# Softmax row sums of an attention kernel: nine of 32 score tiles summed by DMA instead of seven, none directly by TensorE

## The chip, the cores and the metric

The kernel runs on one core of a Trainium2 chip. TensorE does the matrix products into PSUM, ScalarE the exponentials, VectorE additions and copies, GpSimd here issues DMAs that add while they move, SyncE issues the other DMAs. The metric is the device time of one execution in microseconds; the time before is the median of three runs.

## The reference

The input is two images of 256 channels and 64 x 64 positions. Layer 0 is attention with 8 heads of 32 channels over all 4096 positions; layer 1 is a pooled non-local block. The change touches layer 0 alone:

```python
qkv = einsum('oc,bchw->bohw', w_qkv, x)          # q, k, v: (2, 8 heads, 32, 4096)
scores = einsum('bhdi,bhdj->bhij', q, k) / sqrt(32)
attn = softmax(scores, axis=-1)
out = einsum('bhij,bhdj->bhdi', attn, v)
x = einsum('oc,bchw->bohw', w_proj, out) + x      # then layer 1
```

The kernel takes the exponentials without subtracting a maximum, multiplies them with the values, and divides by their sums at the end. The sums over j are what the change is about.

## The kernel before

Layer 0 runs once for each image and each group g of four heads, so four times; call each a stage. In a stage the 4096 query positions are cut into NC = 8 chunks of 512 columns, and the 4096 key positions into JT = 32 tiles of 128 rows. One step makes one score tile of 128 x 2048 (four heads side by side), so there are 256 steps in a stage and 1024 in all.

For each tile TensorE computes the scores (line 372, twelve fp16 products in three terms). The first head goes to the PSUM bank `lead`, the other three to one of two banks of three. ScalarE takes the exponentials in two instructions, line 458 for `lead` and line 459 for the other three, and writes them to one of RING = 8 slots of `P`. TensorE may compute the scores of tile n+2 only when line 458 of tile n+1 has emptied `lead` (line 418). After the scores of each step come four fp32 products a tile with the values (line 381) into the PSUM bank `both`.

The values start late in each chunk, since `both` is used first to make the sums of the chunk before. PV_FROM = 3 says that steps 0, 1 and 2 of a chunk do no values; PV_MORE lists six steps that do three halves of a tile instead of two, so that the values are complete at step 31.

The sums of a chunk are gathered in three ways. VectorE adds 24 tiles into `acc`, in 23 instructions (line 490, the first takes two tiles). The seven tiles of SUM_D are added into `accD` by DMA: GpSimd issues two DMAs a tile, one for each half (k = 0 and 1), the first tile as a plain copy (line 512) and the others with an addition (line 515). Each half waits for the same half of the tile before it (`s_dma[k]`, line 514). GpSimd works in order, so the first half of the next tile is not issued before the second half of this one has been. Tile 31 is not added anywhere. At step 0 of the next chunk TensorE multiplies `acc` with a matrix of ones (line 391), at step 1 tile 31 (line 398), at step 2 `accD` (line 406). Before line 391 VectorE must have copied the finished output out of `both` (line 467, `s_o_free`), and after line 406 it copies the sums to `L` (line 473), before the values of the next chunk may start (`s_l_free`).

ScalarE writes a slot of the ring again eight tiles later. It waits until the values and the adding of the tile are done, for a tile of SUM_D until both its DMAs have landed (lines 440 to 451).

Of the kernel before, what the change touches and what calls it, by code (L numbers as in the profile page):

```python
# [16 lines left out]
HEADS, D = 8, 32  # L17
G = 4
# [3 lines left out]
JT = N // 128  # L22
# [16 lines left out]
RING = 8  # L39
LAG = 2  # L40
SUM_D = [3, 7, 11, 16, 20, 24, 29]
SUM_PE = JT - 1
SUM_V = [j for j in range(SUM_PE) if j not in SUM_D]
ADDS = len(SUM_V) - 1
PV_FROM = 3
PV_MORE = [9, 10, 17, 18, 25, 26]

# [15 lines left out]
def conv_seq(nc, x, wqkv, wproj, gw, tw, pw, ww, vectors, biases, out, r_dram, r1_dram):  # L63
# [3 lines left out]
    with ExitStack() as root:  # L67
# [30 lines left out]
        ones = sb(root, "ones", [128, D])  # L98
# [111 lines left out]
        def layer0(b):  # L210
            with ExitStack() as ctx:
# [8 lines left out]
                for g in range(NG):  # L220
# [123 lines left out]
                    with ExitStack() as c2:  # L344
# [16 lines left out]
                        with nc.Block() as block:  # L361
                            @block.tensor
                            def _(pe):
# [22 lines left out]

                                def sums_of_acc(c):
                                    pe.wait_ge(s_o_free, c + 1)
                                    pe.wait_ge(s_add, (c + 1) * ADDS)
                                    for h in range(G):  # L390
                                        last = nc.tensor.matmul(both[h * D:(h + 1) * D, :], ones[:], acc[:, h, :],  # L391
                                                                start=True, stop=False)
                                    last.then_inc(s_sum, 1)

                                def sums_of_tile(c):
                                    r = (c * JT + SUM_PE) % RING * G
                                    for h in range(G):
                                        last = nc.tensor.matmul(both[h * D:(h + 1) * D, :], ones[:], P[:, r + h, :],
                                                                start=False, stop=False)
                                    last.then_inc(s_sum, 1)  # L400

                                def sums_of_dma(c):
                                    for k in range(2):
                                        pe.wait_ge(s_dma[k], 16 * len(SUM_D) * (c + 1))
                                    for h in range(G):
                                        last = nc.tensor.matmul(both[h * D:(h + 1) * D, :], ones[:], accD[:, h, :],
                                                                start=False, stop=True)
                                    last.then_inc(s_sum, 1)
# [5 lines left out]
                                for n in range(NC * JT + PV_FROM):  # L414
# [5 lines left out]
                                    elif n < NC * JT:  # L420
                                        pe.wait_ge(s_exp, 2 * n + 2)
                                    if i == 0 and c:
                                        sums_of_acc(c - 1)
                                    if i == 1 and c:
                                        sums_of_tile(c - 1)
                                    if i == 2 and c:
                                        sums_of_dma(c - 1)
                                    if c < NC:
# [11 lines left out]
                            def _(act):  # L440
                                def slot_free(m):

                                    c, j = divmod(m, JT)
                                    act.wait_ge(s_pv, m + 1)
                                    if j in SUM_D:
                                        for k in range(2):
                                            act.wait_ge(s_dma[k], 16 * (c * len(SUM_D) + SUM_D.index(j) + 1))
                                    elif j == SUM_PE:
                                        act.wait_ge(s_sum, c * 3 + 2)
                                    else:  # L450
                                        act.wait_ge(s_add, c * ADDS + adds_through(j))
# [12 lines left out]
                            def _(dve):  # L464
# [4 lines left out]
                                def sums_out(c):  # L469
                                    dve.wait_ge(s_sum, (c + 1) * 3)  # L470
                                    if c:
# [3 lines left out]
                                for c in range(NC):  # L475
                                    if c:
                                        output_out(c - 1)
                                    for n in range(ADDS):
                                        j = SUM_V[n + 1]
                                        dve.wait_ge(s_exp, 2 * (c * JT + j) + 2)  # L480
                                        r = (c * JT + j) % RING * G
                                        if n == 0:
                                            if c:
                                                dve.wait_ge(s_sum, (c - 1) * 3 + 1)
                                            r0 = (c * JT + SUM_V[0]) % RING * G
# [4 lines left out]
                                        nc.vector.tensor_tensor(acc[:], old, P[:, r:r + G, :], ALU.add).then_inc(s_add, 1)  # L490
                                        if n == 0 and c:
                                            sums_out(c - 1)
                                        if n == ADDS // 2 and c:
# [7 lines left out]
                            def _(pool):  # L501
                                for c in range(NC):
                                    for i, j in enumerate(SUM_D):
                                        for k in range(2):
# [4 lines left out]
                                            if i == 0:  # L509
                                                if c:  # L510
                                                    pool.wait_ge(s_sum, c * 3)
                                                nc.gpsimd.dma_start(dst, src).then_inc(s_dma[k], 16)  # L512
# [606 lines left out]
```

## Time and profile before

| What | Before |
|---|---|
| median of 3 runs (lowest, highest) | 2709.13 us (2707.6, 2714.66) |
| the profiled execution's own time | 2712.51 us |
| its span in the trace | 2710.8 us |
| TensorE busy | 2553.2 us, 94% |
| ScalarE busy | 2223.1 us, 82% |
| VectorE busy | 2162.7 us, 80% |
| DMA queue of GpSimd, share of 16 engines | 42.7% |

A busy share says how long an engine had an instruction in hand, not that the engine sets the pace. Times are microseconds from the start of the span. In a row of the timeline stand the start, the duration, the engine, the line, the operation, what is written and read, how many instructions were merged (x8), and in brackets how long the engine had stood idle and what ended that. In this kernel a product in fp32 shows as two records, so x8 at line 381 are the four products of one tile. PE is TensorE, DVE VectorE, ACT ScalarE and POOL GpSimd.

### The profile page before, as it was taken

Reading aid. Unit: us, or ns where it says so; the run is one execution under the profiler, and the core shown is the slowest. Engines: PE = TensorE matmul, PEld = TensorE weight load, DVE = VectorE, ACT = ScalarE, POOL = GpSimd, SP = SyncE. Lnnn points to the kernel's source line nnn. Section 1 sums busy time; section 2 is a strip of 40 time slices with the busy share of each in tenths; the row PEclk is TensorE's granted clock in tenths of the full one; section 3 lists DMA queues with packets and bytes.
Section 4 is the critical chain, followed back from the end, with each engine's and each line's share of the span. In section 5 each row is a group of like instructions: output and inputs, shape, how many; then the busy total and the mean of one; then the engine's idle time right before and its main releaser. Section 6 shows DMA issues by size and latency. Waiting matters only on the chain. (4 is left out here: it accounts for less than half of the span.)

```text
span 2710.8 us, 58233 instructions
## 1 busy us (share of the span) xinstructions
PE 2553.2 (94%) x24658; PEld 747.2 (28%) x24666; DVE 2162.7 (80%) x1414; ACT 2223.1 (82%) x2490; POOL 403.5 (15%) x588
## 2 busy tenths in 40 slices
PE   7999999989999999698979999999899999995999
PEld 4222222242222222243442222222422222222434
DVE  3889999948899999586538999999489999994864
ACT  4999999949999999237439999999499999991474
POOL 0111111101111111011001111111011111110100
PEclk9999999999999999899989999999999999998999
DMA  2556666605566566201115665665056656652011
GB/s 83 110 126 126 126 125 127 126 17 110 126 124 127 121 127 126 86 11 48 41 69 117 126 128 121 127 126 121 16 121 124 128 121 127 127 121 79 11 51 43
DMA packets 89277, 272.03 MB, mean 100 GB/s; under 512 B 17504, under 2 KB 18592, under 8 KB 88608
## 3 DMA queue, kind: packets, MB, share of 16 engines
q0 software_dynamic: 64512, 234.91, 42.7%
q1 hardware_dynamic: 24480, 33.16, 3.6%
q8 instruction: 199, 3.26, 0.5%
q14 instruction: 86, 0.70, 0.1%
HBM read 22.88 MB, written 8.68 MB: 12 GB/s over the span
## 5 line engine op out<-in xcount | busy, mean ns | idle before, releaser
L490 DVE TENSOR_TENSOR acc<-acc,P 128x2048 f32<-128x2048 f32 x704 | 1613.4, 2292 | 83.2 <-ACT P L459 15.3
L459 ACT ACTIVATE P<-scores 128x1536 f32<-128x1536 f32 x1024 | 1594.8, 1557 | 0.0
L381 PE MATMUL psOL<-P,V 128*32 128x512 f32 (+1 forms) x8960 | 1074.3, 567 | 1.4 <-ACT P L459 1.4
L372 PE MATMUL psOL<-Q,K 32*128 32x512 f16 x3072 | 842.7, 380 | 28.0 <-ACT P L458 17.3
L372 PE MATMUL scores<-Q,K 32*128 32x512 f16 x9216 | 849.2, 380 | 0.0
L458 ACT ACTIVATE P<-psOL 128x512 f32<-128x512 f32 x1024 | 711.9, 695 | 36.9 <-PE scores L372 36.9
L515 POOL DMA_DIRECT2D accD<-P x384 | 335.7, 998 | 1231.9 <-ACT P L459 1022.4
L372 PEld LDWEIGHTS psOL<-Q,K 32*128 32x128 f16 x3072 | 207.5, 93 | 986.0 <-ACT P L458 855.7
L381 PEld LDWEIGHTS psOL<-P,V 128*32 128x32 f32 x8960 | 196.9, 108 | 474.4 <-issue 438.5
L372 PEld LDWEIGHTS scores<-Q,K 32*128 32x128 f16 x9216 | 220.8, 93 | 0.0
L253 PE MATMUL scores<-X,wq_sb 128*128 128x512 f32 x256 | 128.1, 631 | 40.5 <-DMA X<-in_x 28.1
L512 POOL DMA_DIRECT2D accD<-P x64 | 35.2, 556 | 681.0 <-ACT P L459 398.7
L1039 DVE SCALAR_TENSOR_TENSOR Pl<-O,Ph 128x1536 f16<-128x1536 f32 (+1 forms) x48 | 75.9, 1581 | 65.8 <-ACT Ph L1012 65.8
L490 DVE TENSOR_TENSOR acc<-P 128x2048 f32<-128x2048 f32 x32 | 73.3, 2292 | 64.7 <-PE psOL L391 35.2
L1005 ACT ACTIVATE O<-scores 128x1536 f32<-128x1536 f32 (+1 forms) x48 | 62.4, 1300 | 71.1 <-PE scores L940 71.1
L750 PE MATMUL scores<-O,wp_sb 128*128 128x512 f32 x128 | 62.4, 633 | 49.8 <-DVE O L707 49.8
L739 ACT ACTIVATE Yh<-X 128x512 f16<-128x512 f32 x32 | 20.1, 630 | 104.9 <-DVE X L727 104.9
L952 PE MATMUL psOL<-Ph,GTh 128*128 128x512 f16 x256 | 97.1, 379 | 0.0
L952 PE MATMUL psOL<-Pl,GTh 128*128 128x512 f16 x256 | 97.1, 379 | 0.0
L952 PE MATMUL psOL<-Ph,GTl 128*128 128x512 f16 x256 | 97.1, 379 | 0.0
L253 PEld LDWEIGHTS scores<-X,wq_sb 128*128 128x128 f32 x256 | 51.7, 204 | 100.8 <-issue 70.9
L305 DVE SCALAR_TENSOR_TENSOR Q<-scores,Q 128x512 f16<-128x512 f32 x32 | 22.1, 691 | 66.3 <-ACT Q L284 66.3
(113 smaller groups left out, 1499.3 us busy)
## 6 DMA issues: line engine op xcount, KB each, us to landing
accD<-P POOLq DMA_DIRECT2D x448, 512.0 KB, 5.2
X<-in_x SPq DMA_DIRECT2D x16, 512.0 KB, 7.1
R<-att_inv SPq DMA_DIRECT2D x32, 256.0 KB
out<-res SPq DMA_DIRECT2D x32, 256.0 KB, 2.0
R<-pool_inv SPq DMA_DIRECT2D x2, 2048.0 KB, 7.1
TB<-TA SPq DMA_DIRECT2D x2, 512.0 KB, 4.6
wq_sb<-in_w_qkv SPq DMA_DIRECT2D x1, 768.0 KB, 4.4
Ls<-L SPq DMA_DIRECT2D x32, 8.0 KB
```

Source lines behind the costliest of these rows:

```text
L253: last = nc.tensor.matmul(slot(u), w, X[:, t, c * CH:(c + 1) * CH], start=(t == 0), stop=(t == CT - 1))
L372: last = nc.tensor.matmul(dst[h], K[rows, kp, j * 128:(j + 1) * 128], Q[rows, qp, cs], start=(n == 0), stop=(n == 2))
L381: last = nc.tensor.matmul(both[h * D:(h + 1) * D, lo:hi], V[:, j, h * D:(h + 1) * D], P[:, r + h, lo:hi], start=(j == 0), stop=(j == JT - 1))
L458: nc.scalar.activation(P[:, r, :], lead, ACT.Exp, scale=SCORE).then_inc(s_exp, 1)
L459: nc.scalar.activation(P[:, r + 1:r + G, :], bank[n % 2].rearrange("p (u n) -> p u n", n=CH), ACT.Exp, scale=SCORE).then_inc(s_exp, 1)
L490: nc.vector.tensor_tensor(acc[:], old, P[:, r:r + G, :], ALU.add).then_inc(s_add, 1)
L512: nc.gpsimd.dma_start(dst, src).then_inc(s_dma[k], 16)
L515: nc.gpsimd.dma_start(dst, src, accum_op=ALU.add).then_inc(s_dma[k], 16)
L750: last = nc.tensor.matmul(slot(u), wp_sb[:, k, t * 128:(t + 1) * 128], O[:, k, c * CH:(c + 1) * CH], start=(k == 0), stop=(k == CT - 1))
L952: last = nc.tensor.matmul(psOL[:, t * CH:(t + 1) * CH], w[:, m, ts], v[:, p, m, :], start=(n == 0), stop=(n == 3 * MT - 1))
L1005: nc.scalar.activation(P32[:, p, ms, :], bank[o % 2][:, 0:SZ[k] * CH].rearrange("p (u n) -> p u n", n=CH), ACT.Exp, scale=SCORE1).then_inc ...
L1039: nc.vector.scalar_tensor_tensor(out=Pl[:, p, ms, :], in0=P32[:, p, ms, :], scalar=PS, in1=Ph[:, p, ms, :], op0=ALU.mult, op1=ALU.subtract ...
```

## The change

`SUM_D` has nine tiles now, mostly three apart where they were four or five apart. VectorE adds the other 23 tiles, tile 31 among them, in 22 instructions. TensorE makes two sums between chunks instead of three: `accD` at step 0 and `acc` at step 1. The values start at step 2 and four steps, 9, 10, 19 and 20, carry three halves. VectorE copies the sums to `L` before its first addition of the chunk, where it used to do it after.

```diff
--- before.py
+++ after.py
@@ -38,12 +38,11 @@
 
 RING = 8
 LAG = 2
-SUM_D = [3, 7, 11, 16, 20, 24, 29]
-SUM_PE = JT - 1
-SUM_V = [j for j in range(SUM_PE) if j not in SUM_D]
+SUM_D = [4, 7, 10, 13, 17, 20, 23, 26, 29]
+SUM_V = [j for j in range(JT) if j not in SUM_D]
 ADDS = len(SUM_V) - 1
-PV_FROM = 3
-PV_MORE = [9, 10, 17, 18, 25, 26]
+PV_FROM = 2
+PV_MORE = [9, 10, 19, 20]
 
 
 def adds_through(j):
@@ -384,26 +383,19 @@
                                     if hi == CH:
                                         last.then_inc(s_pv, 1)
 
-                                def sums_of_acc(c):
+                                def sums_of_dma(c):
                                     pe.wait_ge(s_o_free, c + 1)
-                                    pe.wait_ge(s_add, (c + 1) * ADDS)
-                                    for h in range(G):
-                                        last = nc.tensor.matmul(both[h * D:(h + 1) * D, :], ones[:], acc[:, h, :],
-                                                                start=True, stop=False)
-                                    last.then_inc(s_sum, 1)
-
-                                def sums_of_tile(c):
-                                    r = (c * JT + SUM_PE) % RING * G
-                                    for h in range(G):
-                                        last = nc.tensor.matmul(both[h * D:(h + 1) * D, :], ones[:], P[:, r + h, :],
-                                                                start=False, stop=False)
-                                    last.then_inc(s_sum, 1)
-
-                                def sums_of_dma(c):
                                     for k in range(2):
                                         pe.wait_ge(s_dma[k], 16 * len(SUM_D) * (c + 1))
                                     for h in range(G):
                                         last = nc.tensor.matmul(both[h * D:(h + 1) * D, :], ones[:], accD[:, h, :],
+                                                                start=True, stop=False)
+                                    last.then_inc(s_sum, 1)
+
+                                def sums_of_acc(c):
+                                    pe.wait_ge(s_add, (c + 1) * ADDS)
+                                    for h in range(G):
+                                        last = nc.tensor.matmul(both[h * D:(h + 1) * D, :], ones[:], acc[:, h, :],
                                                                 start=False, stop=True)
                                     last.then_inc(s_sum, 1)
 
@@ -420,11 +412,9 @@
                                     elif n < NC * JT:
                                         pe.wait_ge(s_exp, 2 * n + 2)
                                     if i == 0 and c:
+                                        sums_of_dma(c - 1)
+                                    if i == 1 and c:
                                         sums_of_acc(c - 1)
-                                    if i == 1 and c:
-                                        sums_of_tile(c - 1)
-                                    if i == 2 and c:
-                                        sums_of_dma(c - 1)
                                     if c < NC:
                                         at, end = halves_by(i - 1), halves_by(i)
                                         while at < end:
@@ -445,8 +435,6 @@
                                     if j in SUM_D:
                                         for k in range(2):
                                             act.wait_ge(s_dma[k], 16 * (c * len(SUM_D) + SUM_D.index(j) + 1))
-                                    elif j == SUM_PE:
-                                        act.wait_ge(s_sum, c * 3 + 2)
                                     else:
                                         act.wait_ge(s_add, c * ADDS + adds_through(j))
 
@@ -467,7 +455,7 @@
                                     nc.vector.tensor_copy(O[:, g, c * CH:(c + 1) * CH], both).then_inc(s_o_free, 1)
 
                                 def sums_out(c):
-                                    dve.wait_ge(s_sum, (c + 1) * 3)
+                                    dve.wait_ge(s_sum, (c + 1) * 2)
                                     if c:
                                         dve.wait_ge(s_out, 16 * c)
                                     nc.vector.tensor_copy(L[:], both).then_inc(s_l_free, 1)
@@ -475,21 +463,20 @@
                                 for c in range(NC):
                                     if c:
                                         output_out(c - 1)
+                                        sums_out(c - 1)
                                     for n in range(ADDS):
                                         j = SUM_V[n + 1]
                                         dve.wait_ge(s_exp, 2 * (c * JT + j) + 2)
                                         r = (c * JT + j) % RING * G
                                         if n == 0:
                                             if c:
-                                                dve.wait_ge(s_sum, (c - 1) * 3 + 1)
+                                                dve.wait_ge(s_sum, c * 2)
                                             r0 = (c * JT + SUM_V[0]) % RING * G
                                             old = P[:, r0:r0 + G, :]
                                         else:
                                             dve.wait_ge(s_add, c * ADDS + n)
                                             old = acc[:]
                                         nc.vector.tensor_tensor(acc[:], old, P[:, r:r + G, :], ALU.add).then_inc(s_add, 1)
-                                        if n == 0 and c:
-                                            sums_out(c - 1)
                                         if n == ADDS // 2 and c:
                                             dve.wait_ge(s_out, 16 * c)
                                             nc.vector.reciprocal(Ls[:, g, c - 1:c, :], Ls[:, g, c - 1:c, :]
@@ -508,7 +495,7 @@
                                             pool.wait_ge(s_exp, 2 * (c * JT + j) + 2)
                                             if i == 0:
                                                 if c:
-                                                    pool.wait_ge(s_sum, c * 3)
+                                                    pool.wait_ge(s_sum, c * 2 - 1)
                                                 nc.gpsimd.dma_start(dst, src).then_inc(s_dma[k], 16)
                                             else:
                                                 pool.wait_ge(s_dma[k], 16 * (c * len(SUM_D) + i))
```

The order of TensorE's instructions around the first change of chunk, before. Rows at line 372 are scores, L381 values; "..." stands for the other scores.

```order
L381 MATMUL psOL<-P,V 32x512 x4
...
L391 MATMUL psOL<-acc,ones 32x512 [waits s_add,s_o_free]
...
L398 MATMUL psOL<-P,ones 32x512 x4
...
L406 MATMUL psOL<-accD,ones 32x512 [waits s_dma1,s_dma0]
...
L381 MATMUL psOL<-P,V 32x512 [waits s_l_free]
```

And now, where scores are at line 371 and values at line 380:

```order
L380 MATMUL psOL<-P,V 32x512 x4
...
L391 MATMUL psOL<-accD,ones 32x512 [waits s_dma1,s_dma0,s_o_free]
...
L398 MATMUL psOL<-acc,ones 32x512 [waits s_add]
...
L380 MATMUL psOL<-P,V 32x512 [waits s_l_free]
```

The wait for the two DMA semaphores moved from step 2 to step 0, the wait for the last addition from step 0 to step 1, and the product with tile 31 is gone.

VectorE's instructions from the first chunk's additions to the second's, before (`acc<-P` is the first addition of a chunk):

```order
L490 TENSOR_TENSOR acc<-acc,P 128x2048 [waits s_add,s_exp] x22
L467 COPY O<-psOL 128x512 [waits s_pv]
L490 TENSOR_TENSOR acc<-P 128x2048 [waits s_sum,s_exp]
L473 COPY L<-psOL 128x512 [waits s_sum]
L490 TENSOR_TENSOR acc<-acc,P 128x2048 [waits s_add,s_exp] x11
```

And now:

```order
L479 TENSOR_TENSOR acc<-acc,P 128x2048 [waits s_add,s_exp] x21
L455 COPY O<-psOL 128x512 [waits s_pv]
L461 COPY L<-psOL 128x512 [waits s_sum]
L479 TENSOR_TENSOR acc<-P 128x2048 [waits s_sum,s_exp]
L479 TENSOR_TENSOR acc<-acc,P 128x2048 [waits s_add,s_exp] x11
```

One addition a chunk is gone, and the copy to `L` now stands ahead of the first one.

## Rows read from the trace of the kernel before

**Rows 1.** The page: busy time of each engine, and the DMA queues.

```profile
PE 2553.2 (94%) x24658; PEld 747.2 (28%) x24666; DVE 2162.7 (80%) x1414; ACT 2223.1 (82%) x2490; POOL 403.5 (15%) x588
q0 software_dynamic: 64512, 234.91, 42.7%
```

**Rows 2.** Two chunks: stretch, length, busy time of each engine, clock, DMA.

```profile
137.45:197.32 59.87, 59.73 (x696) 13.70 (x688) 54.11 (x27) 59.13 (x65) 11.62 (x14) 1.00 0.62 125
197.32:257.19 59.87, 59.73 (x696) 13.68 (x688) 54.12 (x27) 59.13 (x65) 11.67 (x14) 1.00 0.61 125
```

**Rows 3.** Timeline of ScalarE over a change of chunk and a pair of long steps.

```profile
187.36 1.50 ACT L459 ACTIVATE P<-scores 128x1536 f32<-128x1536 f32 x1
190.49 0.69 ACT L458 ACTIVATE P<-psOL 128x512 f32<-128x512 f32 x1
...
194.11 0.74 ACT L458 ACTIVATE P<-psOL 128x512 f32<-128x512 f32 x1
...
203.14 0.87 ACT L458 ACTIVATE P<-psOL 128x512 f32<-128x512 f32 x1
...
208.61 0.90 ACT L458 ACTIVATE P<-psOL 128x512 f32<-128x512 f32 x1
...
212.98 0.60 ACT L458 ACTIVATE P<-psOL 128x512 f32<-128x512 f32 x1 [0.25 <-PE scores L372]
```

**Rows 4.** Timeline of TensorE over the same change of chunk.

```profile
190.16 1.07 PE L381 MATMUL psOL<-P,V 128*32 128x512 f32 x8
...
192.04 1.06 PE L391 MATMUL psOL<-acc,ones 128*32 128x512 f32 x8
193.07 0.39 PE L372 MATMUL psOL<-Q,K 32*128 32x512 f16 x1
...
193.82 1.07 PE L398 MATMUL psOL<-P,ones 128*32 128x512 f32 x8
```

**Rows 5.** Timeline of VectorE over the same change of chunk.

```profile
183.04 7.08 DVE L490 TENSOR_TENSOR acc<-acc,P 128x2048 f32<-128x2048 f32 x3
191.29 0.69 DVE L467 COPY O<-psOL 128x512 f32<-128x512 f32 x1 [1.17 <-PE psOL L381]
```

**Rows 6.** Timeline of GpSimd: tile 29, then tiles 16 and 20 later.

```profile
185.49 1.77 POOL L515 DMA_DIRECT2D accD<-P  x2 [7.25 <-ACT P L459]
...
280.58 1.75 POOL L515 DMA_DIRECT2D accD<-P  x2 [7.81 <-ACT P L459]
287.96 0.86 POOL L515 DMA_DIRECT2D accD<-P  x1 [5.63 <-ACT P L459]
289.71 0.87 POOL L515 DMA_DIRECT2D accD<-P  x1 [0.89 <-DMA accD<-P]
```

**Rows 7.** Issue to landing: tile 29 of two chunks, a late second half, all L512.

```profile
DMA to landing us min/median/max: 4.6/5.6/6.6
DMA to landing us min/median/max: 4.6/6.3/8.1
DMA to landing us min/median/max: 6.1/6.1/6.1
DMA to landing us min/median/max: 2.9/3.9/6.1
```

**Rows 8.** Two stretches that each hold one tile's pair of adding DMAs.

```profile
212.40:218.40 6.00, 6.00 (x76) 1.33 (x72) 5.79 (x3) 5.75 (x7) 0.50 (x1) 1.00 0.95 180
222.00:228.00 6.00, 5.99 (x80) 1.57 (x76) 5.90 (x4) 5.80 (x7) 0.47 (x1) 1.00 0.96 179
```

**Rows 9.** Timeline of the end of the last stage.

```profile
2437.02 1.75 POOL L515 DMA_DIRECT2D accD<-P  x2 [7.83 <-ACT P L459]
2444.32 1.07 PE L406 MATMUL psOL<-accD,ones 128*32 128x512 f32 x8
2445.44 0.69 DVE L473 COPY L<-psOL 128x512 f32<-128x512 f32 x1 [3.18 <-PE psOL L406]
```

## The prediction

> **What bounds the kernel now.** I read the busy shares first, then two chunks side by side, then ScalarE's timeline, then the other engines' across one change of chunk, and last the DMAs that GpSimd issues. TensorE is busy 94% of the span and ScalarE 82% [rows 1], which does not yet say which of them sets the pace. Inside a stage the chunks repeat to the hundredth: 59.87 us each, TensorE busy 59.73, ScalarE 59.13, VectorE 54.1 [rows 2]. ScalarE's start of line 458 is the beat. From 190.49 to 203.14 it beats seven times, 1.807 us a step, with no idle time named [rows 3]: ScalarE is the bound, and this stretch holds all three sums of the chunk before. 32 such steps are 57.83 us, so a chunk has 2.04 us beyond ScalarE's pace. They come from the long steps: over one pair ScalarE goes from 208.61 to 212.98, 4.37 us for two steps, and the idle time there is ended by the scores [rows 3]. Three pairs share the 2.04 us, 0.68 us a pair (the pair shown loses 0.76, a little of which comes back after it). So TensorE counts in the long steps and at the change of chunk if something holds it there, and nowhere else.
>
> **What the change takes away.** One pair of long steps goes: 32 chunks x 0.68 = 21.8 us. The product with tile 31 goes as well, 1.07 us in the records [rows 4]. It gives nothing between chunks, because it lies in a step without values, under ScalarE's beat of 1.807; at the end of each stage, where nothing covers it, it is worth about 1 us, and I count it in the tail below. VectorE loses one addition a chunk, 2.36 us (7.08 for three) [rows 5]. It has 5.8 us idle a chunk already (59.87 less 54.1) and gives nothing directly.
>
> **What it moves: the wait for the DMA.** The product with `accD` stood at step 2 and stands at step 0. Tile 29, the last one of SUM_D, is the same tile as before. Its DMAs were issued at 185.49, when ScalarE had finished it [rows 6], and the product that stood at step 0 began at 192.04 [rows 4], 6.55 us later. Nothing makes ScalarE finish tile 29 earlier relative to step 0. So the question is when tile 29's second half lands. It is issued 0.88 us behind the first (1.77 us for two issues) [rows 6] and lands 6.6 us after its issue in the shortest usual case and 8.1 in the longer one [rows 7]; over the 32 tiles 29 of the trace the mean is 7.1, the two rows being examples of the two kinds (16 of 32 are at 6.6 to 6.8, 12 at 7.2 to 8.3). That is 7.5 us after the first issue at the usual best and 8.0 on the mean, against the 6.55 us at which TensorE arrives. A new stall at step 0 is 1.45 us on the mean even if the DMAs never queue.
>
> Of that stall ScalarE has little to give. At 194.11 line 458 takes 0.74 us where one that waited takes 0.60 [rows 3]: some 0.15 us of reserve. TensorE's own order has none, since the next scores follow the sum at once (192.04 + 1.03 = 193.07) [rows 4], and ScalarE's later steps run at its own pace, so nothing is caught up. Behind the waiting product on TensorE stand the scores of tile 3; for these waits ScalarE, and for ScalarE everything. Cost without queueing: 1.3 us a change of chunk, and 0.8 if every landing is at 7.5.
>
> **What it adds: a tighter chain of DMAs.** The tiles of SUM_D were 4 or 5 steps apart, 7.2 us or more; now seven of the eight gaps are 3 steps, 5.42 us, and two of those (10 to 13, 20 to 23) hold a pair of long steps, 6.1 us. What can the DMA engines do? In the two stretches of 6.00 us, each around one tile's two adding DMAs, the engines' share is 0.95 and 0.96 [rows 8]: 5.7 us of all 16 engines a tile, at 180 GB/s. As a cross-check, the queue's 42.7% of 2710.8 us is 1157 us for 192 adding tiles and 32 plain ones [rows 1]; at 2.6 for a plain one, taken as half, 5.6 remain for an adding one. A gap of 5.42 against a service of 5.6 means that the DMAs are never ahead. Tile 13 to 17 (7.2 us) clears what has gathered; after it come 17, 20, 23, 26, 29. With a service of 5.6 the lag at tile 29 is 0.3 us. The longer landings weigh more: on the mean a second half takes 0.5 us over the usual 6.6. If that is engine time the service is 6.1, and the lag is 0.7 + 0 + 0.7 + 0.7, about 2.0 us. The trace has cases of a late second half: at 289.71 it is issued 1.75 us behind the first half instead of 0.88 and lands in 6.1 [rows 6, 7], where a pure queue of 5.6 would make it 5.7. So part of the extra remains under queueing, and I take 1.0 us, the middle of 0.3 and 2.0. That gives 1.3 + 1.0 = 2.3 us a change of chunk, with ends of 0.8 and 3.3; there are 7 changes in each of four stages, 28 in all: 64 us, ends 22 and 92.
>
> A page of the Trainium skill speaks against this. "DMA: Bandwidth & Descriptors", section "Anatomy of one DMA — SWDGE (gpsimd) path", gives 2.0 us and the bytes at 436 GB/s for a DMA issued by GpSimd, which for 512 KB is an estimate of 3.2 us. The plain copies agree with it at their shortest (2.9 us), the adding ones do not (4.6 us and more) [rows 7]. By the page both halves would be home long before step 0, and the sum would be the second rival's; by the rows it is mine.
>
> **VectorE at the change of chunk.** Now the last addition is tile 31's. It can start only when tile 30's is done: ScalarE finishes tile 31 at 188.86 (187.36 + 1.50) and tile 30 a step earlier, at 187.05 [rows 3], two additions end at 187.05 + 4.7 = 191.8, the copy of the output takes 0.7 more, and the product could start at 192.5 instead of 192.04. VectorE will not be further behind than that: its additions start right behind the copy to `L`, 22 x 2.36 + 0.3 = 52.2 us after it, and a chunk is 59.2 us or longer. This 0.45 us lies under the wait for the DMA (ready 1.4 us late or more). If that cover is gone it costs 0.3 us a chunk after ScalarE's reserve. The new place of the copy to `L` costs nothing: it follows the last sum by the same 0.1 us and the values wait for it as before, one step earlier. The ring: tile 29's slot is needed 7 steps, 12.6 us, after its exponentials, and the landing with lag is at 8.9, up to 9.9.
>
> **Ends of stages.** In the last stage tile 29 is issued at 2437.02, the last sum begins at 2444.32, the copy to `L` ends at 2446.13 [rows 9]. Now the landing is at 2437.0 + 8.9 = 2445.9, then come two products (2.0 us) and the copy (0.8): 2448.7, 2.6 us later, ends 1.2 and 3.6. Four stages: +10 us, ends 5 and 14.
>
> **Sum.** -21.8 + 64 + 10 = +53 us. The profiled execution took 2712.5 (span 2710.8); it would take 2766. It lies 3.4 us above the median of the runs, so in medians: 2709.1 + 53 = 2762 us, ends 2709 - 22 + 22 + 5 = 2714 and 2709 - 22 + 92 + 14 = 2793.
>
> **Rivals.**
> First, *landings at their best*. Every second half lands 6.6 us after its issue and queueing absorbs the rest: 0.8 us a change, +22 + 5 - 22, so 2714 us, no change. For it: half of the tiles 29 land so. Against it: three in eight take 0.6 us more or longer, and the next tiles come sooner.
> Second, *the DMA is home in time*, faster. If a half that is issued alone or in a steady chain lands in under 5.5 us, the product at step 0 waits only for VectorE: -22 + 28 x 0.3 = -13, 2696 us. It decides if the landing is under 6.7 us after tile 29's first issue; no pair in the trace does it. This is also what the page's figure would give.
> Third, *the chain becomes the bound*, slower still. If each second half needs its full 6.6 us from issue to landing, however the halves are staggered, the lag grows 1.2 us a gap (0.5 where long steps lie) and from tile 17 on reaches about 4.2 us, some 5.3 if the plain gap does not clear it: 1.3 + 4.2 to 5.3, or 6 us a change, 168 - 22 + 25, 2880 us. For it: second halves issued late still take 6.1 us. Against it: they take less than 6.6, and the share of 0.95 says that the engines work through.
>
> **Chances and range.** The forecast, with its own range 2718 to 2800 (the ends of the sum, less the first rival's own place): 0.70. First rival 0.12, second 0.07, third 0.11. What a measurement of this kernel can tell from no change is about 0.3%, 8 us. The forecast, the third rival and a small part of the first (over 2717) are slower: 0.83; same 0.10; faster 0.07. The range that holds 8 in 10 leaves out the second rival and most of the third: 2710 to 2825.
>
> **What would show it.** TensorE's product with `accD` idles before it, ended by the DMA, 1 to 3 us in 28 places, and ScalarE has an equal gap ended by scores once a chunk; a chunk is 61.5 us instead of 59.87. GpSimd's waits at line 502 (the old 515) are ended by the DMA most of the time. ScalarE's gaps at long steps are 4 a chunk, not 6. If no idle time stands before the product, or if the chunk is 59.2 us, my landing time is wrong; if the chunk is over 64 us, the third rival is right. A stall ended by the output's copy would make VectorE the cause.

## The result, and the profile after

| | Before | After |
|---|---|---|
| median | 2711.89 us (4 runs, 2707.6 to 2714.97) | 2806.62 us (4 runs, 2801.51 to 2808.12) |
| ratio to before, 95% interval | | 1.0347 (1.0332 to 1.0361) |
| span of the profiled execution | 2710.8 us | 2805.7 us |
| mean granted clock | 0.983 | 0.968 |

The kernel is 94.7 us slower. The prediction was 2762 us with a range to 2825: the direction holds and so does the main cause, a wait for the DMA at step 0, but the loss is nearly twice as large as the 53 us forecast.

The page of the kernel after, with the busy times, the DMA queue and the groups that answer to the argument (busy us, mean ns, then idle time before them and what ended it):

```profile
PE 2563.2 (91%) x24146; PEld 735.5 (26%) x24154; DVE 2086.7 (74%) x1382; ACT 2221.8 (79%) x2490; POOL 511.0 (18%) x716
q0 software_dynamic: 82944, 302.03, 54.0%
L446 ACT ACTIVATE P<-psOL 128x512 f32<-128x512 f32 x1024 | 706.5, 690 | 109.9 <-PE scores L371 109.9
L461 DVE COPY L<-psOL 128x512 f32<-128x512 f32 x32 | 22.1, 691 | 190.0 <-PE psOL L398 190.0
L391 PE MATMUL psOL<-accD,ones 128*32 128x512 f32 x256 | 43.8, 760 | 90.1 <-DMA accD<-P 90.1
```

VectorE has less to do than before [rows 1]. TensorE idles 90.1 us in front of the product with `accD`, ended by the DMA every one of 32 times. ScalarE waits 109.9 us for scores; before it was 36.9:

```profile
L458 ACT ACTIVATE P<-psOL 128x512 f32<-128x512 f32 x1024 | 711.9, 695 | 36.9 <-PE scores L372 36.9
```

Two neighbouring chunks, to be read beside [rows 2]:

```profile
141.16:203.89 62.73, 60.43 (x680) 13.30 (x672) 51.56 (x26) 59.08 (x65) 15.03 (x18) 0.97 0.76 152
203.89:265.12 61.23, 58.95 (x680) 13.17 (x672) 51.74 (x26) 59.09 (x65) 15.02 (x19) 1.00 0.78 156
```

Before, 24 of the 28 changes of chunk came 59.87 us after the one before; only the first of each stage took longer, 62.3 us on the mean. Now they differ, and the longer one of the two shown has a granted clock of 0.97. On the mean of all 28 (each measured from one chunk's first DMA issue to the next one's, the three steps from one stage to the next left out) a chunk takes 62.68 us now and took 60.21 before, 2.47 more: 69 us. The four ends of stages are 16.2 us longer in all. The last 9.5 us of the 94.9 between the two spans lie in what is left of the first and last chunks and outside the stages; I can't place them.

The changes of chunk in these two, first on ScalarE, then on TensorE:

```profile
194.45 0.87 ACT L446 ACTIVATE P<-psOL 128x512 f32<-128x512 f32 x1
...
199.82 0.60 ACT L446 ACTIVATE P<-psOL 128x512 f32<-128x512 f32 x1 [3.16 <-PE scores L371]
...
257.18 0.87 ACT L446 ACTIVATE P<-psOL 128x512 f32<-128x512 f32 x1
...
261.05 0.60 ACT L446 ACTIVATE P<-psOL 128x512 f32<-128x512 f32 x1 [1.65 <-PE scores L371]
```

```profile
196.44 1.93 PE L391 MATMUL psOL<-accD,ones 128*32 128x512 f32 x8 [2.07 <-DMA accD<-P]
198.30 0.60 PE L371 MATMUL psOL<-Q,K 32*128 32x512 f16 x1
...
259.17 1.06 PE L391 MATMUL psOL<-accD,ones 128*32 128x512 f32 x8 [2.07 <-DMA accD<-P]
```

TensorE idles 2.07 us both times. But ScalarE's step of 1.81 us becomes 5.37 us the first time (from 194.45 to 199.82) and 3.87 the second (from 257.18 to 261.05). The difference, 1.50 us, lies behind the idle time, and it is the difference between the two chunks above: at 196.44 the product takes 1.93 us instead of 1.06 and the scores' matmuls 0.60 instead of 0.39. The stretches around it show the granted clock (third number from the end):

```profile
194.00:196.00 2.00, 0.37 (x8) 0.00 (x0) 0.65 (x2) 2.00 (x3) 0.00 (x0) 1.00 0.88 164
196.00:198.00 2.00, 1.56 (x8) 0.23 (x8) 0.00 (x0) 0.66 (x1) 0.00 (x0) 0.59 0.00 0
198.00:200.00 2.00, 2.00 (x20) 0.46 (x20) 0.00 (x0) 0.18 (x1) 0.00 (x0) 0.56 0.00 0
200.00:202.00 2.00, 1.94 (x24) 0.38 (x20) 1.15 (x2) 2.00 (x3) 0.00 (x0) 1.00 0.03 8
```

For most of 196 to 200 the array runs at the lower of its two levels, 1.2 GHz instead of 2.4. TensorE had been idle for about 2 us when it fell, but the second change of chunk had the same idle time and kept 1.00: the length of the idle time alone does not decide. The clock shows below 1.00 around 14 of the 28 changes of chunk (the expectation of e1_cover below says 15, a miscount). The Trainium skill ("TensorE: Matmul & The Clock Gate", the section on the HAM clock gate) says that the clock falls when the array has been idle and comes back with sustained work; the trace agrees on that, with each of the 14 falls at such a stall or just behind it.

Tile 29's DMAs at this change of chunk. ScalarE finishes the tile at 187.50, GpSimd issues the halves at 188.38 and 191.72:

```profile
185.89 1.61 ACT L447 ACTIVATE P<-scores 128x1536 f32<-128x1536 f32 x1
```

```profile
188.38 0.87 POOL L502 DMA_DIRECT2D accD<-P  x1 [2.58 <-ACT P L446]
191.72 0.87 POOL L502 DMA_DIRECT2D accD<-P  x1 [2.46 <-ACT P L446]
```

```profile
DMA to landing us min/median/max: 4.6/4.6/4.6
```

And before, the exponentials of tile 29, then its second half alone:

```profile
183.74 1.45 ACT L459 ACTIVATE P<-scores 128x1536 f32<-128x1536 f32 x1
186.02 1.23 POOL L515 DMA_DIRECT2D accD<-P  x1
```

The second half is issued 4.2 us after the exponentials, where it was 0.8 (186.02 against 185.19), and lands 4.6 us later, at 196.3, 8.8 us after them. That is an early case: over the 28 changes of chunk it lands 8.5 to 10.25 us after them, 9.3 on the mean, where it was 8.0 before. (The names in brackets are the last event before the issue; with ScalarE's tile done 4 us before, what GpSimd really waited for must be the same half of tile 26.)

The end of the last stage, to be read beside [rows 9]:

```profile
2527.63 1.66 ACT L447 ACTIVATE P<-scores 128x1536 f32<-128x1536 f32 x1
...
2534.69 1.93 PE L391 MATMUL psOL<-accD,ones 128*32 128x512 f32 x8 [4.29 <-DMA accD<-P]
2536.37 1.80 PE L398 MATMUL psOL<-acc,ones 128*32 128x512 f32 x8
2538.24 0.69 DVE L461 COPY L<-psOL 128x512 f32<-128x512 f32 x1 [5.47 <-PE psOL L398]
```

The last exponential before:

```profile
2438.89 1.50 ACT L459 ACTIVATE P<-scores 128x1536 f32<-128x1536 f32 x1
```

From the end of the last exponential to the sums in `L` it takes 9.6 us. Before it was 5.7 (2440.39 to 2446.13). The four ends of stages grew by 3.9 to 4.3 us. In this one, too, both products run at the lower clock.

### The profile page after: what moved, and what is told of

The parts are those of the page before. It is cut to its first block and busy times, and to the rows that moved or that the text cites. A ratio compares the mean times of both kernels' runs of the same rounds, so it can differ in the third digit from the quotient of the medians.

```text
span 2805.7 us, 57433 instructions
## 1 busy us (share of the span) xinstructions
PE 2563.2 (91%) x24146; PEld 735.5 (26%) x24154; DVE 2086.7 (74%) x1382; ACT 2221.8 (79%) x2490; POOL 511.0 (18%) x716
## 5 line engine op out<-in xcount | busy, mean ns | idle before, releaser
L479 DVE TENSOR_TENSOR acc<-acc,P 128x2048 f32<-128x2048 f32 x672 | 1540.3, 2292 | 173.7 <-ACT P L447 119.1
L446 ACT ACTIVATE P<-psOL 128x512 f32<-128x512 f32 x1024 | 706.5, 690 | 109.9 <-PE scores L371 109.9
L502 POOL DMA_DIRECT2D accD<-P x512 | 443.2, 887 | 1166.5 <-ACT P L447 599.7
L380 PEld LDWEIGHTS psOL<-P,V 128*32 128x32 f32 x8704 | 184.8, 108 | 465.1 <-issue 431.8
L499 POOL DMA_DIRECT2D accD<-P x64 | 35.2, 557 | 729.1 <-ACT P L447 729.1
L461 DVE COPY L<-psOL 128x512 f32<-128x512 f32 x32 | 22.1, 691 | 190.0 <-PE psOL L398 190.0
L391 PE MATMUL psOL<-accD,ones 128*32 128x512 f32 x256 | 43.8, 760 | 90.1 <-DMA accD<-P 90.1
```

The costliest lines, as they stand in the source:

```text
L380: last = nc.tensor.matmul(both[h * D:(h + 1) * D, lo:hi], V[:, j, h * D:(h + 1) * D], P[:, r + h, lo:hi], start=(j == 0), stop=(j == JT - 1))
L446: nc.scalar.activation(P[:, r, :], lead, ACT.Exp, scale=SCORE).then_inc(s_exp, 1)
L502: nc.gpsimd.dma_start(dst, src, accum_op=ALU.add).then_inc(s_dma[k], 16)
```

## The experiments

The first four form a square, seven sparse or nine dense DMA tiles with the product of `accD` at step 0 or step 1, with one run beside it that tests the clock. The square is not quite clean: with seven tiles VectorE makes one addition more, and tile 31 is in no sum. Each ratio compares with the kernel before on the same chip.

| Run | DMA tiles | accD at step | Median, us | Ratio to before (95%) |
|---|---|---|---|---|
| after | 9, dense | 0 | 2806.62 | 1.0347 (1.0332 to 1.0361) |
| e1_gaps | 7, sparse; tile 31 left out | 0 | 2731.05 | 1.0064 (1.0047 to 1.0081) |
| e1_swap | 9, dense | 1 | 2724.10 | 1.0043 (1.0029 to 1.0057) |
| e1_pair | 7, sparse; tile 31 left out | 1 | 2701.33 | 0.9957 (0.9943 to 0.9972) |
| e1_cover | 9, dense | 0, with filler work | 2778.34 | 1.0243 (1.0226 to 1.0260) |
| e2_eight | 8, gaps 4 and 3 | 1 | 2706.94 | 0.9978 (0.9969 to 0.9988) |
| e2_third_pair | as e2_eight, with extra products | 1 | 2720.43 | 1.0028 (1.0017 to 1.0039) |
| e2_single | as e2_eight, long steps apart | 1 | 2698.11 | 0.9944 (0.9927 to 0.9961) |
| e3_early | 7, before's | 0 | 2771.46 | 1.0209 (1.0191 to 1.0226) |
| e3_no_product | 7, before's; most of tile 31 left out | 2 | 2713.35 | 0.9999 (0.9987 to 1.0010) |

### e1_gaps: the sparse tiles of before, the wait at step 0

```diff
-SUM_D = [4, 7, 10, 13, 17, 20, 23, 26, 29]
-SUM_V = [j for j in range(JT) if j not in SUM_D]
+SUM_D = [3, 7, 11, 16, 20, 24, 29]
+SUM_V = [j for j in range(JT - 1) if j not in SUM_D]
```

Expected: 

> The changed kernel with the seven DMA tiles of the kernel before (3, 7, 11, 16, 20, 24, 29), four or five steps apart; tile 31 is in no sum, so VectorE still makes 23 additions and the sums lack one tile. The product with accD stays at step 0. Theory: tile 29's second half lands about 8.0 us after its first issue as in the kernel before, TensorE arrives at about 6.6 to 6.9, so it idles about 1.2 us a change of chunk instead of 2.6, and the clock falls seldom. 28 x 1.3 - 21.8 + 8 for the ends of stages gives about 2735 us. Rival (the wait is all lag of the denser chain): no stall at step 0, about 2690 us.

Measured 2731.05 us. The groups line of the product:

```profile
L391 PE MATMUL psOL<-accD,ones 128*32 128x512 f32 x256 | 36.2, 636 | 42.7 <-DMA accD<-P 42.7
```

42.7 us of idle time instead of 90.1; over the changes of chunk it is 0.67 to 2.15 us each, 1.1 on the mean, never under 0.67. So the place of the product alone costs a wait, as the landing times of before said, and the density of the chain adds 1.5 us to each. The clock is 1.00 around every change of chunk. Fewer tiles, with tile 31 left out, take 75.6 us off the time after.

### e1_pair: the same with the products exchanged

```diff
-                                        sums_of_dma(c - 1)
-                                    if i == 1 and c:
                                         sums_of_acc(c - 1)
+                                    if i == 1 and c:
+                                        sums_of_dma(c - 1)
```

(The start and stop flags, the wait for the output's copy and GpSimd's first wait move along.) Expected: 

> As e1_gaps (seven DMA tiles four or five apart, tile 31 in no sum), but with the two products exchanged: acc at step 0, accD at step 1. Theory: the DMA has 1.8 us more, no stall above 0.2 us a change of chunk, and what is left is the pair of long steps that went (28 to 32 x 0.68) and one product less at the ends of stages: about 2688 us. Rival (the pair of long steps was not worth 0.68 us a chunk, other waits take its place): 2705 to 2712 us.

Measured 2701.33 us, between theory and rival. The DMA wait is gone, but the gain is 11.1 us and not over 20. The trace says where it stays. ScalarE, deep in a stretch without long steps:

```profile
195.88 0.90 ACT L446 ACTIVATE P<-psOL 128x512 f32<-128x512 f32 x1
...
205.05 0.90 ACT L446 ACTIVATE P<-psOL 128x512 f32<-128x512 f32 x1
```

Five steps take 9.17 us, 1.834 each, not 1.807. The duration of this instruction (line 458 before, 446 here) grows by some 0.03 us a step from 0.60 [rows 3] up to 0.90, and then the step is 1.834: I read this as TensorE's loop setting the pace, since the scores wait for the end of that instruction. No run made that loop shorter, so this is a reading of the trace; e2_third_pair tests what follows from it. Each wait of ScalarE puts the duration back to 0.60 and gives some 12 faster steps, 12 x 0.027 = 0.33 us, a reserve that a wait renews. So a chunk's floor is 32 x 1.834 = 58.69 us, and a pair of long steps costs 4.37 us [rows 3] less two such steps, 0.70, less the 0.33 that come back: about 0.4. With two pairs that makes 59.5 (most chunks of this run are 59.47), with three 59.9 (59.87 before).

### e1_swap: the kernel after with the products exchanged alone

The edit of e1_pair, on the kernel after. Expected: 

> The changed kernel with its nine DMA tiles, only the two products exchanged: acc at step 0, accD at step 1. Theory: the landing stays where it was, 2.6 us after TensorE's old arrival on the mean, TensorE arrives 1.8 us later, so 0.8 us of stall are left a change of chunk, too short for the clock to fall, plus 0.2 for VectorE's later last addition: -22 + 28 x 1.0 + 8 for the ends, about 2725 us. Rival (the chain bounds the chunk as a whole): the chunk stays at 62.7 us and the time near 2800.

Measured 2724.10 us:

```profile
L390 PE MATMUL psOL<-accD,ones 128*32 128x512 f32 x256 | 37.1, 652 | 18.0 <-DMA accD<-P 17.9
```

Moving one wait by one step takes 82.5 us off the time after. The landings stay where they were (9.4 us after the exponentials on the mean). The chain is as dense as before the exchange, so the chain as such does not bound the chunk (60.19 us on the mean); what bounds is the time at which its last landing is asked for. The stall left is 0.56 us on the mean of 28 where I expected 0.8, but up to 1.99, and behind that one the clock fell. The chain's density (with tile 31's addition) costs 22.8 us here (against e1_pair) and 75.6 us where the product stands at step 0: the two parts of the change are not additive.

### e1_cover: filler work in the wait

```diff
                                     pe.wait_ge(s_o_free, c + 1)
+                                    pe.wait_ge(s_add, (c + 1) * ADDS)
+                                    for _ in range(2):
+                                        for h in range(G):
+                                            nc.tensor.matmul(both[h * D:(h + 1) * D, :], ones[:], acc[:, h, :],
+                                                             start=True, stop=True)
                                     for k in range(2):
```

Expected: 

> The changed kernel with eight more products a change of chunk (ones with acc, twice four, about 1.8 us of work whose result is overwritten), after the output's copy is seen and before the wait for the DMA. Theory: the DMA lands when it did; TensorE idles under 1.5 us, the granted clock stays at 1.00 around the product where it fell in 15 of 28 changes of chunk, and the 14 us in the gap itself and some 10 to 15 behind it come back: about 2780 us although work was added. Rival (the clock falls for another reason, or the slow steps behind the product are not what costs): 2806 us or a little more.

Measured 2778.34 us: with 256 more products the kernel is 28.3 us faster than the kernel after. The first stretch of 8 us below is the kernel after's around its second change of chunk, with the clock down; the other is this kernel's around its own:

```profile
193.00:201.00 8.00, 5.92 (x56) 1.10 (x52) 1.80 (x3) 4.84 (x6) 0.00 (x0) 0.79 0.35 66
```

```profile
193.00:201.00 8.00, 7.95 (x96) 1.74 (x92) 5.40 (x4) 6.62 (x8) 1.10 (x2) 1.00 0.19 70
```

In this kernel no change of chunk within a stage shows a clock below 1.00. A chunk takes 61.90 us, 0.79 less than after. The wait for the DMA is still there, filled: the product with `accD` starts 9.49 us after tile 29's exponentials on the mean, against 9.46 in the kernel after. So what came back is what followed it, 22 us between chunks and 3.7 at the ends of stages. This is the clock's share of the loss, shown by work added and not by work left out.

### e2_eight: eight DMA tiles, everything computed

```diff
-SUM_D = [4, 7, 10, 13, 17, 20, 23, 26, 29]
+SUM_D = [4, 8, 11, 15, 18, 22, 25, 29]
```

with the edit of e1_swap. Expected: 

> The changed kernel with eight DMA tiles in gaps of four and three (4, 8, 11, 15, 18, 22, 25, 29), VectorE adding the other 24, and the two products exchanged (acc at step 0, accD at step 1). Everything is computed. Theory: each gap of four clears the lag of the gap of three before it, tile 29 comes after a gap of four, so the landing is about 8 us after its issue and the product at step 1 hardly waits; VectorE's 23 additions end with tile 31 as late as in e1_gaps and cost 0.1 a chunk. So about e1_pair, 2702 us (2697 to 2708). Rival (the dense chain lags whatever the pattern): near e1_swap, 2720 us.

Measured 2706.94 us. Most chunks are at 59.50, as in e1_pair, and the idle time before the product is 1.0 us in all. So alternating gaps of four and three steps are slow enough for the chain. The 5 to 6 us over e1_pair are at the ends of stages: from the last exponential to the sums in `L` the four of them take 30.3 us, in e1_pair 24.9. There tile 31's addition, which e1_pair leaves out, now stands ahead of the output's copy.

### e2_third_pair: what a pair of long steps costs

```diff
                                                 at += 2
+                                        if i in (26, 27):
+                                            values(c, j, 0, CH // 2)
```

Expected: 

> As e2_eight, but at steps 26 and 27 of each chunk the first half of the tile just done is multiplied with its values once more and added to the output again (the output is wrong by that), which makes a third pair of long steps. Theory from e1_pair's chunk of 59.47: between waits ScalarE runs at 1.807 until TensorE's loop of 1.833 has eaten its reserve, so a pair costs its 0.74 less the 0.34 that come back, 0.40 us a chunk: 32 x 0.40 = 13 us over e2_eight. Rival (my first reading, 0.68 a pair): 22 us.

Measured 2720.43 us, 13.5 more than e2_eight. The first issues of two neighbouring chunks, 59.90 us apart:

```profile
196.15 1.09 POOL L501 DMA_DIRECT2D accD<-P  x2 [10.88 <-ACT P L449]
...
256.05 1.09 POOL L501 DMA_DIRECT2D accD<-P  x2 [11.26 <-ACT P L449]
```

Against 59.49 or 59.50 in e2_eight that is 0.41 us a pair. The rival's 0.68 is out.

### e2_single: the long steps apart

```diff
-PV_MORE = [9, 10, 19, 20]
+PV_MORE = [6, 14, 22, 30]
```

Expected: 

> As e2_eight, but the four steps with three halves stand alone (6, 14, 22, 30) instead of in pairs. Theory: four waits of 0.37 with 8 steps of reserve between them (8 x 0.026 = 0.21) cost 0.64 a chunk where two pairs cost 0.80, so 5 us less than e2_eight, if a step whose two halves belong to two tiles costs no more than one with a whole tile. Rival: such a step is longer by more than 0.03 us (eight products of 256 columns instead of four of 512), 16 of them a chunk, and TensorE's loop, not ScalarE, then sets their length: 15 us or more over e2_eight.

Measured 2698.11 us, 8.8 less than e2_eight. A chunk at its usual length:

```profile
255.80 1.09 POOL L499 DMA_DIRECT2D accD<-P  x2 [11.32 <-ACT P L447]
...
314.94 1.10 POOL L499 DMA_DIRECT2D accD<-P  x2 [10.16 <-ACT P L447]
```

59.14 us. ScalarE's wait for scores falls from 29.0 to 17.4 us. A step whose halves belong to two tiles costs no more that shows. The gain is 0.35 us a chunk where I expected 0.16, so my account of the reserve has the direction right and misses half of the size. This is the fastest version, everything is computed, and it beats both kernels: 0.56% under the kernel before.

### e3_early: the kernel before with its products in another order

```diff
                                     if i == 0 and c:
-                                        sums_of_acc(c - 1)
+                                        sums_of_dma(c - 1)
                                     if i == 1 and c:
-                                        sums_of_tile(c - 1)
+                                        sums_of_acc(c - 1)
                                     if i == 2 and c:
-                                        sums_of_dma(c - 1)
+                                        sums_of_tile(c - 1)
```

(The flags and waits move along.) Expected: 

> The kernel before with its order of products changed alone: accD at step 0, acc at step 1, tile 31 at step 2; seven DMA tiles, three pairs of long steps, nothing left out. Theory: tile 29 lands 0.7 us or more after TensorE reaches step 0, as in e1_gaps (mean idle 1.1 us), of which 0.3 comes back in ScalarE's pace; with the ends of stages that is the 29.7 us between e1_gaps and e1_pair: 2713 + 20 to 30, about 2738 us. Rival (the wait matters only together with the new steps): 2713 us.

Measured 2771.46 us, 57 us over before: a miss by 30 us. The wait for the DMA is as expected (0.67 to 2.2 us), but a second wait stands two steps behind it. VectorE, then TensorE:

```profile
194.78 2.29 DVE L490 TENSOR_TENSOR acc<-P 128x2048 f32<-128x2048 f32 x1 [3.75 <-PE psOL L390]
196.99 0.68 DVE L473 COPY L<-psOL 128x512 f32<-128x512 f32 x1
```

```profile
197.73 1.06 PE L381 MATMUL psOL<-P,V 128*32 128x512 f32 x8 [0.57 <-DVE L L473]
```

With `acc` read at step 1, VectorE's first addition starts a step later, and the copy to `L` waits behind it; the values of the new chunk wait for that copy. Where the wait for the DMA is at its shortest, 0.7 us, a chunk is 60.65; with that wait alone it would be some 60.2 (59.87 + 0.67, less the 0.31 of the reserve). So the second wait costs some 0.4 us a chunk, about 12 of the 30 us missed. The ends of stages take some 6 us more than I reckoned with, and the rest I leave to the clock, below 1.00 at four changes of chunk; no run tests this split. The change under study moves that copy ahead of the addition and so avoids the second wait.

### e3_no_product: tile 31's product cut to 8 columns

```diff
-both[h * D:(h + 1) * D, :], ones[:], P[:, r + h, :],
+both[h * D:(h + 1) * D, 0:8], ones[:], P[:, r + h, 0:8],
```

Expected: 

> The kernel before with the product of tile 31 cut to 8 of its 512 columns (the sums lack most of that tile); the step, its place and the three pairs of long steps stay. Theory: nothing between chunks, since the step lies under ScalarE's pace, and about 0.9 us at each of four ends of stages: 2710 us, 3 to 4 less than the kernel before. Rival (TensorE's work at the change of chunk counts): 0.85 us in each of 28 changes more, about 2686 us.

Measured 2713.35 us, ratio 0.9999 (0.9987 to 1.0010), and chunks of 59.86 and 59.87 but for the first of each stage. The product that the change set out to remove was worth nothing between chunks. It was worth nothing at the ends of stages either, where I had expected 0.9 us each: the product with `accD` can't start earlier there, since it now waits for the DMA.

```profile
L406 PE MATMUL psOL<-accD,ones 128*32 128x512 f32 x256 | 34.1, 604 | 2.8 <-DMA accD<-P 2.8
```

All of the 2.8 us are at the four ends; before, there were 0.2.

## Why the prediction was right in kind and short in size

**The bound.** ScalarE's pace of 1.807 was read right in the stretch shown, but it isn't the floor. The rows already held the slower one: the three steps from 203.14 to 208.61 take 5.47 us, 1.823 each [rows 3]. The floor is a loop of 1.834 with a reserve of 0.33 us that every wait renews (e1_pair, e2_third_pair).

**The pair of long steps: mis-sized.** I divided everything above ScalarE's pace among three pairs, 0.68 each. It is 0.40 (e2_third_pair: 0.41). The gain over 32 chunks is 13 us and not 21.8. "A little of which comes back after it" stood in the prediction and was left unpriced.

**The product with tile 31.** Nothing between chunks, as predicted; nothing at the ends of stages, where 1 us was predicted (e3_no_product).

**The wait for the DMA: right, with luck in its size.** Predicted was an idle time of 2.45 us at step 0; the mean of 28 is 2.59 us (1.77 to 3.52). But its two parts were both off, in opposite ways. Without lag I had 1.45, and e1_gaps shows 1.1: I took half of the 1.77 us of both issues, 0.88, as the distance of the second half from the first, but the second is issued 0.54 us behind it (186.02 against 185.49), and 0.54 + 7.1 - 6.55 = 1.1. For the chain's lag I had taken 1.0, the middle of 0.3 and 2.0, and it is 1.5 (2.59 against 1.1). The reserve gives back 0.3 and not 0.15.

The Trainium skill ("DMA: Bandwidth & Descriptors", section "Anatomy of one DMA — SWDGE (gpsimd) path") has a figure for a DMA from GpSimd under which there would be no wait. For adding DMAs of this size it is out: in both kernels none landed in under 4.5 us, and even the sparse chain of e1_gaps never landed in time.

**The clock: missing.** Every stretch that I read stood at 1.00, and the sum had no term for what an idle TensorE does to its own next microseconds. The step that failed is the price of the stall: "1.3 + 1.0 = 2.3 us a change of chunk" took the idle time for the whole cost. e1_cover puts the missing part at 28 us, 22 of them between chunks (28 x 0.79). The chunks of the kernel after say the same by themselves, the first change of each stage left out. A chunk's length less its idle time is 59.2 us in the 13 chunks where the clock stayed up, as in all 24 of e1_gaps; it is 60.5 to 60.7 in 8 where the clock fell and 61.6 to 61.9 in 3 where it stayed down longer. That is 0.81 us a chunk on the mean.

**The ends of stages.** 2.6 us each were predicted, 3.9 measured at the last one and 4.1 on the mean of four, the surplus in part again from two products at the lower clock.

**The sum as it stands.** For each of the 24 changes of chunk that are not the first of a stage: pair -0.40 (59.87 to e1_pair's 59.47), reserve -0.31 (59.47 to 59.16, a chunk of e1_gaps less its idle time), idle +2.54, clock +0.81, together 2.64 of the measured 2.65. The first ones grew by 1.41 us. 24 x 2.65 + 4 x 1.41 + 16.2 = 85 us of the 94.9 between the spans; 9.5 us stay unplaced, and the sum never had a term for them.

**VectorE's later last addition** lay under the DMA's wait as predicted; VectorE's copy of the output ended about 1.8 us before the product began (194.65 against 196.44):

```profile
193.97 0.68 DVE L455 COPY O<-psOL 128x512 f32<-128x512 f32 x1
```

**The rivals.** Landings at their best (first) and home in time (second) are refuted by an idle time that is never below 1.77 us. The third, each half needing 6.6 us from its issue however staggered, is refuted too: a late second half landed in 4.6 us, and the median of all adding DMAs fell from 6.0 to 5.3 us although the queue is fuller. The chain works through; it is only asked too early. Before, then after:

```profile
DMA to landing us min/median/max: 4.5/6.0/8.3
DMA to landing us min/median/max: 4.5/5.3/8.0
```

**The signs.** The chunk of 61.5 us came out at 62.5 to 62.7. ScalarE's gaps at long steps are two a chunk and were three, one a pair; the prediction said 4 and 6. Of GpSimd's 465 waits at line 502 the profile puts 131 down to the DMA and 130 to line 446, behind which, as above, there may be a DMA; "most of the time" is not shown.

## What to carry to other kernels

Before moving a wait earlier, measure when the awaited thing is really there relative to the new place, over all its cases and from the start of each single issue; with the issue read right, the mean landing of the trace before gives the wait of e1_gaps to within 0.1 us. A stall of TensorE can cost a clock drop on top. Here the clock fell at 14 of 28 stalls of 1.8 to 3.5 us, at 0.8 us a stall on the mean of all, and filler products in the wait brought that back where the wait itself couldn't be removed. Where two engines wait for one another each step, a long step is cheaper after enough normal ones: e2_single, with its four long steps apart, was faster than e2_eight with two pairs.

## What the runs showed that I had not expected

- Of two stalls of the same 2.07 us one was followed by 4 us at a clock near 0.6 and the other was not. In the kernel after a stall of 3.01 us went by without a fall, and in e1_swap the clock fell behind one of 1.99 us. Around the changes of chunk of e1_gaps, with stalls of 0.67 to 2.15 us, the clock never fell.
- 256 added fp32 products made a kernel 1% faster (2778.34 against 2806.62 us).
- ScalarE's instruction on the bank `lead` takes 0.60 us after a wait and up to 0.90 in a full pipeline, while the step stays at 1.81 to 1.83 us. The work is the same, so I take the difference for waiting that no idle column shows; here it is a gauge of the reserve that is used up.
